# Message phase of a four-layer graph network: places as repeated bytes, degrees in VectorE's comparisons, half of the filter loads from ScalarE

## What is computed

```python
# layer 1, attention: softmax over the edges of each dst, weighted sum of h[src]
# layer 2:
xn = node @ Wn
f = ssp(edge @ We1 + be1) @ We2 + be2        # "filter", one row of 128 for each edge
msg = xn[edge_index[1]] * f                   # edge_index[1] is dst
agg = segment_sum(msg, edge_index[0])         # summed by src
return node + (ssp(agg @ W2 + b2) @ W3 + b3)
# layer 3: deg = segment_sum(1, dst) + 1; out = segment_sum(h[src] / sqrt(deg[src] * deg[dst])) + b
```

## Time and profile before

| | us |
|---|---|
| runs (three), median | 5773.97 |
| runs, lowest and highest | 5771.99, 5784.74 |
| profiled execution, its own time | 5730.71 |
| profiled execution, its span | 5728.9 |
| attention phase in it | 140 to about 1500 |
| message phase in it, first to last start of L1112 | 1565.8 to 2035.2 |
| all that follows (three layers of gathers and sums) | 2036 to the end |

### The profile page before, as it was taken

The page is one execution under the profiler, slowest core; times in us unless marked ns, Lnnn a source line. Parts: engine busy times, 40 slices in busy tenths (PEclk is TensorE's granted clock), DMA queues, the critical chain, the costliest instruction groups (busy, mean ns, idle before and its releaser), DMA issues.

```text
span 5728.9 us, 57142 instructions
## 1 busy us (share of the span) xinstructions
PE 2748.0 (48%) x14121; PEld 2218.5 (39%) x14121; DVE 2627.2 (46%) x7265; ACT 1433.5 (25%) x4291; POOL 3546.7 (62%) x3833
## 2 busy tenths in 40 slices
PE   2677777777588833333343413333333233333334
PEld 2455556555466623333332313222323222332333
DVE  6687767775655523333333423333333323333333
ACT  2685556555577710000000100000000000000000
POOL 2666656666255566666666466666666566666664
PEclk8898888888677755555656655555555556555555
DMA  6565556556177731111111111111111111111111
GB/s 140 139 154 139 140 130 147 139 136 148 44 231 236 230 90 45 49 50 48 49 50 48 35 47 50 49 49 49 49 50 48 40 47 48 50 49 50 49 48 37
DMA packets 433201, 490.37 MB, mean 86 GB/s; under 512 B 88331, under 2 KB 335327, under 8 KB 432870
## 3 DMA queue, kind: packets, MB, share of 16 engines
q0 software_dynamic: 131904, 288.49, 19.4%
q1 hardware_dynamic: 296424, 194.27, 12.6%
q10 hardware_dynamic: 4542, 3.90, 0.3%
HBM read 359.63 MB, written 126.70 MB: 85 GB/s over the span
## 4 chain that ended last, share of the span: by engine, by line
another core or an unknown queue 33%; issue 19%; PE 18%; DVE 16%; ACT 8%; DVEq 4%; DMA 1%; ACTq 0%; POOL 0%; POOLq 0%; SPq 0%
DVE acc L996 9%; PE bank L1775 4%; PE bank L1701 4%; DVEq L771 2%; ACT arena L1269 2%; PE bank L1618 2%; PE bank L1608 2%; PE bank L1626 2%; ACT arena L1153 1%; ACT arena L1281 1%; DVEq L768 1%; ACT arena L1283 1%; DVE arena L1036 1%; PE bank L1688 1%
## 5 line engine op out<-in xcount | busy, mean ns | idle before, releaser
L1796 POOL DMA_INDIRECT arena<-node_table,pick x1664 | 1612.4, 969 | 847.7 <-issue 486.3
L1775 PE MATMUL bank<-arena 128*128 128x128 f32 x4992 | 1149.1, 404 | 1998.5 <-DVE arena L1036 1413.1
L1775 PEld LDWEIGHTS bank<-arena 128*128 128x128 f32 x4992 | 1003.0, 298 | 2166.8 <-DVE arena L1036 1520.8
L996 DVE TENSOR_TENSOR acc<-acc,bank 128x128 f32 x2496 | 719.2, 288 | 2434.2 <-remote 1784.9
L1796 POOL DMA_INDIRECT arena<-gat_table,pick x832 | 856.4, 1029 | 530.0 <-issue 219.5
L1796 POOL DMA_INDIRECT arena<-message_table,pick x832 | 805.5, 968 | 378.7 <-issue 240.4
L1036 DVE TENSOR_TENSOR arena<-iota_free,local 128x512 f32<-128x512 f32 x624 | 430.3, 690 | 0.7
L1369 ACT ACTIVATE rstd<-moments,eps_col 128x4 f32<-128x4 f32 (+2 forms) x39 | 11.6, 297 | 1456.1 <-issue 1053.1
L1388 ACT COPY arena<-acc 128x128 f32 x98 | 22.1, 294 | 1407.2 <-DVE acc L996 1137.7
L1701 PE MATMUL bank<-arena 128*128 x1664 | 331.6, 362 | 57.8 <-DVE arena L1120 57.6
L1701 PEld LDWEIGHTS bank<-arena 128*128 128x128 f32 x1664 | 284.6, 259 | 123.3 <-issue 123.3
(11 more groups left out here) (271 smaller groups left out, 3711.3 us busy)
## 6 DMA issues: line engine op xcount, KB each, us to landing
message_table<-arena POOLq DMA_DIRECT2D x208, 256.0 KB, 3.4
filter_table<-arena SPq DMA_DIRECT2D x196, 256.0 KB
arena<-filter_table SPq DMA_DIRECT2D x624, 64.0 KB
xt<-edge_cols SPq DMA_DIRECT2D x131, 256.0 KB
arena<-local_rows SPq DMA_DIRECT2D x208, 128.0 KB
arena<-node_table,pick POOLq DMA_INDIRECT x1664
arena<-edge_cols SPq DMA_DIRECT2D x65, 256.0 KB
arena<-gat_table,pick POOLq DMA_INDIRECT x832
```

What stands on the lines that cost most here:

```text
L996: e.tensor_tensor(a, a, bank[6 + t % 2][:, s * P:(s + 1) * P], ALU.add).then_inc(sums, 1)
L1775: ins = e.matmul(bank[6 + n % 2][:, s * P:(s + 1) * P], hot[n % 2][:, s, :], gathered[:, slot(n, s), 0:D], start=True, stop=True)
L1796: e.indirect_dma_start(out=dst, out_offset=None, in_=table, in_offset=bass.IndirectOffsetOnAxis(ap=index, axis=0)).then_inc(done, 16)
```

## The change

It does five things:

1. `local_rows`, `local_row` (attention phase) and `local_in` (message phase) hold bytes (U8) and not bf16.
2. In the message phase GpSimd loads the places of four ticks repeated over 128 partitions (2 KB in each, 256 KB in all) instead of 4 KB into one. It asks one loop turn earlier, and waits for comparisons (`m_hot`) instead of spreading products. The spreading product, its ones and its semaphore are gone, and picking products n come in TensorE's turn n.
3. VectorE's comparison becomes four of 128x128 from bytes in SBUF, each of which also leaves its sum in `degree_part` (`accum_out`). ScalarE's sums are gone. VectorE's turn t is message t - 3, then the comparisons of tick t.
4. ScalarE issues the last two filter loads of a tick and SyncE the first two; GpSimd issues none. ScalarE starts on them after its last copy before the phase (L1337).
5. The message waits for one filter semaphore instead of two.

```diff
-        local_rows = dram("local_rows", [SW * P], BF16)
+        local_rows = dram("local_rows", [SW * P], U8)
-        local_row = [part([P, GRP * P], BF16) for _ in range(3)]
+        local_row = [part([P, GRP * P], U8) for _ in range(3)]
-        local_in = [part([1, LT * GRP * P], BF16) for _ in range(2)]
+        local_in = [part([P, LT * GRP * P], U8) for _ in range(2)]
 # VectorE
-            for t in range(TICKS + 4):
-                n = t - 4
+            for t in range(TICKS + 3):
+                n = t - 3
                 if n >= 0:
                     e.wait_ge(m_spread, n + 1)
                     e.wait_ge(f_in[n % FT], f_value(n))
-                    e.wait_ge(ring[n % RT], last_filter_value(n))
...
-                    e.tensor_scalar(hot_n[n % HN][:, :], bank[2 + n % 2][:, :], iota_part[:, 0:1], None, ALU.is_equal
-                                    ).then_inc(m_hot, 1)
+                    for s in range(GRP):
+                        at = (n % LT * GRP + s) * P
+                        i = e.tensor_scalar(hot_n[n % HN][:, s * P:(s + 1) * P], local_in[n // LT % 2][:, at:at + P],
+                                            iota_part[:, 0:1], 0.0, ALU.is_equal, ALU.add,
+                                            accum_out=degree_part[:, n * GRP + s:n * GRP + s + 1])
+                    i.then_inc(m_hot, 1)
 # ScalarE
             for n in range(TICKS):
-                e.wait_ge(m_hot, n + 1)
-                for s in range(GRP):
-                    i = n * GRP + s
-                    if i:
-                        e.wait_ge(degree_added, i)
-                    e.activation(hot_copy[:, :], hot_n[n % HN][:, s * P:(s + 1) * P], ACT.Copy,
-                                 accum_out=degree_part[:, i:i + 1]).then_inc(degree_added, 1)
+                if n >= FT:
+                    e.wait_ge(m_made, n - FT + 1)
+                if n % 4 == 0:
+                    e.load(starts, start_row[:, n * GRP:n * GRP + 16])
+                for s in range(GRP // 2, GRP):
+                    at = e.snap(starts[(n * GRP + s) % 16], min_val=0, max_val=2 * EW - P)
+                    e.dma_start(filter_in[n % FT][:, s, :], filter_table[bass.ds(at, P), :]
+                                ).then_inc(f_in[n % FT], 16)
 # TensorE
-                    e.matmul(bank[2 + n % 2][:, :], ones_row[:, :],
-                             local_in[n // LT % 2][:, n % LT * GRP * P:(n % LT + 1) * GRP * P], start=True, stop=True
-                             ).then_inc(m_places, 1)
 # GpSimd
-                e.dma_start(local_in[b % 2][:, :], flat_local[:, b * LT * GRP * P:(b + 1) * LT * GRP * P]
+                e.dma_start(local_in[b % 2][:, :],
+                            flat_local[:, b * LT * GRP * P:(b + 1) * LT * GRP * P].to_broadcast([P, LT * GRP * P])
                             ).then_inc(l_in[b % 2], 16)
-                if t % LT == 2 and 1 < t // LT + 1 < TICKS // LT:
+                if t % LT == 1 and 1 < t // LT + 1 < TICKS // LT:
-                    if n + FT < TICKS:
-                        last_filters_in(n + FT)
 # SyncE
-                for s in range(GRP - 1):
+                for s in range(GRP // 2):
```

More of the change, by code:

```diff
@@ L159, in part @@
                 free *= n
-            words = -(-free * (2 if dt == BF16 else 4) // 4)
+            words = -(-free * {BF16: 2, U8: 1}.get(dt, 4) // 4)
             at = taken[0]
@@ L352, in build_program @@
         l_in = [sem(f"places_in{k}") for k in range(2)]
-        m_places, m_hot, m_spread, m_made = (sem("message_" + n) for n in ("places", "hot", "spread", "made"))
+        m_hot, m_spread, m_made = (sem("message_" + n) for n in ("hot", "spread", "made"))
         m_out = [sem(f"message_out{k}") for k in range(MT)]
@@ L400, in f_value @@
             k = n % FT
-            return 16 * (len(range(k % 3, FTICKS if k < 3 else TICKS, 3)) + (GRP - 1) * (n // FT + 1))
+            return 16 * (len(range(k % 3, FTICKS if k < 3 else TICKS, 3)) + GRP * (n // FT + 1))
         def sum_place(t, s):
@@ L1347, in scalar @@
                     root(n, means_made, roots_made)
+            e.wait_ge(start_in, 80)
+            starts = [e.register(f"start_reg_a{k}").__enter__() for k in range(16)]
             for n in range(TICKS):
-                e.wait_ge(m_hot, n + 1)
-                for s in range(GRP):
-                    i = n * GRP + s
-                    if i:
-                        e.wait_ge(degree_added, i)
-                    e.activation(hot_copy[:, :], hot_n[n % HN][:, s * P:(s + 1) * P], ACT.Copy,
-                                 accum_out=degree_part[:, i:i + 1]).then_inc(degree_added, 1)
+                if n >= FT:
[6 more added lines that the diff above has]
+                                ).then_inc(f_in[n % FT], 16)
             e.wait_ge(degree_summed, 1)
@@ L1861, in places_in @@
                 if b > 1:
-                    e.wait_ge(m_places, (b - 1) * LT)
-                e.dma_start(local_in[b % 2][:, :], flat_local[:, b * LT * GRP * P:(b + 1) * LT * GRP * P]
+                    e.wait_ge(m_hot, (b - 1) * LT)
+                e.dma_start(local_in[b % 2][:, :],
+                            flat_local[:, b * LT * GRP * P:(b + 1) * LT * GRP * P].to_broadcast([P, LT * GRP * P])
                             ).then_inc(l_in[b % 2], 16)
-            starts = [e.register(f"start_reg_g{k}").__enter__() for k in range(16)]
-            def last_filters_in(n):
-                if n % 4 == 0:
-                    e.load(starts, start_row[:, n * GRP:n * GRP + 16])
-                at = e.snap(starts[(n * GRP + GRP - 1) % 16], min_val=0, max_val=2 * EW - P)
-                e.dma_start(filter_in[n % FT][:, GRP - 1, :], filter_table[bass.ds(at, P), :]
-                            ).then_inc(ring[n % RT], 16)
             places_in(0)
@@ L1881, in gpsimd @@
             e.wait_ge(win_taken, 8)
-            for n in range(FT):
-                last_filters_in(n)
             for t in range(TICKS + 4):
-                if t % LT == 2 and 1 < t // LT + 1 < TICKS // LT:
+                if t % LT == 1 and 1 < t // LT + 1 < TICKS // LT:
                     places_in(t // LT + 1)
```

38 lines of the change are left out of this document (12 added, 26 removed).

## The result

The changed kernel takes 5686.4 us (median of 4 runs, 5681.3 to 5690.9) where the kernel before takes 5773.0 (4 runs, 5766.7 to 5784.7). The profiled execution took 5690.5 us, its span is 5688.3.

A forecast was written before the change was run, and what follows sets the result against it. TensorE was taken to lead the message phase at 2.27 us a tick. A tick of 2.0 gives -55 us and the attention phase +3, so 5774 - 52 = 5722 us, range 5680 to 5790.

The forecast's parts named there:

- rival 5: Message phase: more gain than forecast, comparison 0.25 us, tick 1.8, attention phase faster by smaller loads; 5670 us; chance 0.09.
- The spreading product goes: Message phase, TensorE's path: 208 products go, 0.53 us each at 1.2 GHz, 0.31 at 2.4; slow tick becomes 2.1.
- VectorE's comparison: Message phase: four comparisons with sums at 0.32 us each (0.21 to 0.39), read included; VectorE's tick 1.88 us (1.44 to 2.16).
- The tick after: Message phase: half the time TensorE's 2.1, half VectorE's 1.88, rounded up to 2.0 us; 55 us less over 207 ticks.
- rival 4: Message phase: TensorE stays at 1.2 GHz; all ticks at 2.1 give 5742, the slow end at 2.5 gives 5825, chance 0.05.
- The DMA engines: Message phase: DMA work grows from 1.66 to 1.9 us a tick, 95% of a tick of 2.0; 0.19 from the places.
- rival 2: Message phase: DMA engines become the bound at a share of 0.84, tick 2.26 us, 5777 us, no change; chance 0.12.
- The split of the loads: Message phase, filter loads on SyncE and ScalarE: worth 0 by itself, but keeps a new wait away, three loads being 1.94.
- ScalarE's sums: Message phase: four a tick, off the path but for the buffer's wait; two DMA issues replace them, 1.3 us, under 2.0.
- GpSimd, and the start: Message phase: GpSimd's changed loads cost 0; ScalarE's first loads take 4 to 6 us, first message where it was, 0.
- The attention phase: Attention phase: comparison on bytes takes 0.48 us, +0.13 a tick; 5 us on the path less 2 for smaller loads, +3 us.
- Rival 3: Attention phase: byte comparison at one element a cycle, 0.39 us more a tick, 82 us; kernel slower at 5801; chance 0.12.

The follow-up runs named there:

- few_places: Changed kernel, but GpSimd loads only the first two of 52 blocks of places and comparisons reuse them (wrong places): 4957.6 us, ratio 0.982 to the kernel before, tick 1.71 us.
- attention_bytes: Kernel before with only the attention phase's places as bytes, from a table of their own: 5775.9 us against 5779.7, ratio 0.999 (0.998 to 1.000).
- sync_all: Changed kernel with all four filter loads on SyncE, none on ScalarE or GpSimd: 5798.9 us, ratio 1.011 to the kernel before, tick 2.54 us.
- gpsimd_fourth: Changed kernel with filter loads as before, three of SyncE and the fourth of GpSimd: 5683.7 us, ratio 0.990 to the kernel before, tick 2.01 us.
- no_sums: Changed kernel with one 512-column comparison a tick and no degrees summed: 5643.7 us, ratio 0.983 to the kernel before, tick 1.80 us.
- after_again: The changed kernel once more, unchanged: 5673.8 us, ratio 0.983 (0.980 to 0.985) to the kernel before.

## Why the prediction was right, and where it was off

**The number, first.** 5686.4 lies in the range by 6 us. It lies below the forecast's own spread (5694 to 5745), and nearer to the 5670 of rival 5, a tick of 1.8 with a chance of 0.09, than to 5722. Three of my signs of being right failed, all to the fast side: 374.5 us from first to last message (390 to 435), comparisons at 0.265 us (0.3 to 0.35), a share of 1.02 (0.85 to 0.95). That the time stayed in the range is in part luck: my step for VectorE was too slow, and the transfers, which I had not made the bound, took part of that back. At the 1.71 us of few_places it would be, as an estimate, 21 us less, 5665, below the range.

**The spreading product goes, and TensorE with it: right.** The wait for picking products fell from 190.9 us to 3.3. The register load's hole, for which I kept 0.1 us a tick, reaches VectorE hardly any more: all its waits for TensorE are 3 in 207 ticks.

**VectorE's comparison: the step of the read was too dear.** I took 0.27 + 0.05 = 0.32; it is 0.265 and 0.00. The bounds 0.21 to 0.39 held. VectorE's tick is 1.66 instead of 1.88. The sum of 0.21 and 0.065 for the operation was right to a hundredth; its parts no run measures apart. The read doesn't cost a start even where the next operation sums as well.

**The tick after: this term was mis-sized.** 2.0 was forecast, with 1.88 to 2.1 as its spread, and 1.81 measured: 0.19 us x 207 = 39 us, which covers the distance between the forecast gain of 52 us and the measured 87. Two steps made it. The one is VectorE's 0.22 above. The other is that half of the ticks stay at TensorE's slow pace of 2.1. The granted clock rose from 0.73 to 0.91, which is 82% of the time at 2.4 GHz rather than half, and VectorE waited for TensorE only 3.3 us in all, so the slow stretches were evened out. I had kept the clock of before for an engine whose work and waits both change; rival 4, a fall to 1.2 GHz, went the wrong way.

**The DMA engines: the work was right, the ceiling wrong.** 1.9 us of work a tick were forecast, and a share of 1.02 over 1.81 us is 1.85. For rival 2, I had taken the highest share in any 5 us of the trace of before, 0.84, as a candidate for the most that can be had. It was demand, not a limit: 1.02 is had over 300 us. But the mechanism of rival 2 is what sets the tick now, at 1.80 rather than 2.26. The 0.19 us that the bytes add are a real price: without sums, leaving the places out gives 0.14 of it back (1.80 to 1.66); with them only 0.10, where VectorE holds the rest. By the Trainium skill (DMA: Bandwidth & Descriptors, Where 436 GB/s comes from) these bytes were an estimated 1.65 us; the runs moved 328 GB/s where the page has about 358 between the memory and one core, so the measurement decides for 1.80.

**The split of the loads: wrong.** I put it at 0 by itself, since three loads (1.94) fit into a tick of 2.0, and said that without it they would come close to the new tick. They are over it: 1.9 us against 1.81, and the kernel without the split has a tick of 2.01, 42 us more in the message phase. How much of the 0.20 is SyncE's queue and how much the fourth load in GpSimd's stays open. It is nearly half of the gain, and the part that I had called the one expected to do nothing. The mistake follows from the mis-sized tick: an issuer with 0.06 us of slack on an estimate with a spread of 0.2 is not off the path.

**ScalarE's sums: right.** To move them is worth 0.02 us a tick by itself, measured where the filter loads held the tick at 2.0.

**GpSimd, and the start: right in sum.** VectorE waited 0.8 us for places in all, and from the last attention comparison to the first message it is 85.4 and 85.1 us, against 87.5 and 86.7. But the start is not as forecast. VectorE stood idle 0.8 us before the first comparison, where it was 8.0 us for the spreading product; most of that is given back in the 6.95 us in which the first message waits for filters. ScalarE's last copy ends at 1579.73 us, not near the first comparison (1572.96), and the first message follows 3.5 us behind it. The 4 to 6 us for that, which no row had shown, were a little too much.

**The attention phase: right.** 0.48 us was forecast for the comparison on bytes, 0.482 measured, and +3 us for the phase; attention_bytes gives -4 us, with -12 to +1 as its interval. A fifth of the 27 us on the path was, if anything, too much on a chip of that sort; on the quick one (last section) no run tells. Rival 3 (0.74 us) fell. The rule of the Trainium skill (VectorE: DVE Perf Modes, What auto-detection actually checks), that a single source in SBUF of another size than 16 bits gets half the highest rate, agrees with the trace: 132 ns more, where by it an estimated 133 were due. My test in the trace, the phase's end within 10 us, failed in the first pair (19.5) and held in the second (-0.4): one pair of executions doesn't carry it.

**The profiled execution: right to keep its distance.** It was 43 us under its median, of which about 30 lay behind the message phase (3693.7 us against 3719 to 3731). The difference of the profiles (40.6 us) would have halved the gain; the medians give 87.

## What to carry to other kernels

When one resource of a loop is removed, work out the next three limits to the same precision, issue queues among them, before calling a part worthless: here TensorE's 2.25 gave way to 2.01 with the filter loads unsplit, then to the transfers' 1.80, with VectorE at 1.71 just behind. A full engine beside a full DMA share is told apart by taking away one of them at a time. A peak in a trace tells what was asked, not what can be had; and a difference of two single profiles should be divided by phase, with the phases that nobody touched as its error bar.

## What the runs showed of the hardware

**The accumulator's read is free in a sequence.** DVE_READ_ACCUMULATOR shows 83 ns (832 of them), and in the ticks of the timeline the next comparison, or the message behind the fourth, starts with it.

**Bytes and sums on VectorE.** 512 columns from bytes without a sum took 0.48 us, from bf16 0.35. With a sum, a comparison of 128 columns starts every 0.265 us.

**The share of the DMA engines can read over 1.** 1.02 to 1.03 at 325 to 330 GB/s, for loads of 64 KB in packets of some 450 bytes and writes of 256 KB. The write of a message took 5.3 us to land where it was 3.4 in before.

**The clock doesn't follow TensorE's busy share in one direction.** Over 300 us of the message phase: granted 0.74 at 86% busy and a tick of 2.27 (before), 0.69 at 64% and 2.54 (sync_all), 0.82 at 67% and 2.01 (gpsimd_fourth), 0.91 at 68% and 1.81 (after), 0.85 at 70% and 1.80 (no_sums). Nor does the length of the tick give it: the last two have the same tick. The row of sync_all:

```profile
1600.00:1900.00 300.00, 191.85 (x921) 171.52 (x920) 198.90 (x1036) 0.00 (x0) 77.72 (x144) 0.69 0.75 228
```

**Chips differ, and not by one factor.** On one chip the kernel before took 5040.0 us instead of 5736.7 to 5779.7. The message tick was the same there, 1.81 us. What was shorter were the phases that gather rows by GpSimd: the last stretch took 3222 us instead of 3723. A gather itself cost nearly the same (956 and 969 ns); the idle time before it shrank by 314 us, and the 274 us that the profile puts down to "remote", a releaser that it doesn't name further, are no longer among its largest. GpSimd's gathers of the last stretch on that chip, and on the one of after_again (busy us, mean ns, idle before):

```profile
L1783 POOL DMA_INDIRECT arena<-node_table,pick x1664 | 1591.0, 956 | 553.0 <-issue 506.1 <-DMA node_table<-acc 32.9 <-DMA node_table<-x_sb 13.3
```

```profile
L1783 POOL DMA_INDIRECT arena<-node_table,pick x1664 | 1612.4, 969 | 866.6 <-issue 477.8 <-remote 274.2 <-DMA node_table<-acc 66.3
```

On that chip the change was worth 57 us (ratio 0.989), against 87 to 102 on the others, at the same message tick after. What took the rest is open. An attention tick is 5.53 us there instead of 6.5, and VectorE is busy 88% instead of 78% in that phase, so that the byte comparison's 27 us would be the first suspect; attention_bytes ran only on a chip of the other sort, where it costs nothing.
